# A two-layer graph transformer block on one core: row norms made chunk by chunk in the stages where their rows arise, the graph weight applied ahead of the aggregation, the output stored by chunks

## The reference

```python
xn = _layernorm(x)
x = x + _L0_gnn_ref(xn, src, dst, Wq, bq, Wk, bk) + _L0_mix_ref(xn, ...)
x = x + _L0_ffn_ref(_layernorm(x), ...)
xn = _layernorm(x)
x = x + _L1_gnn_ref(xn, edge_weight, W, b, src, dst) + _L1_mix_ref(xn, ...)
x = x + _L1_ffn_ref(_layernorm(x), ...)

def _L0_mix_ref(x, ...):            # t: linear attention over all rows
    x1 = layer_norm(t + x, ln1_g, ln1_b)
    h = gelu(x1 @ W1.T + b1)
    return layer_norm(h @ W2.T + b2 + x1, ln2_g, ln2_b)

def _L1_gnn_ref(x, edge_val, W, b, edge_row, edge_col):
    support = x @ W
    gathered = support[edge_col] * edge_val[:, None]
    return segment_sum(gathered, edge_row) + b

def _L1_mix_ref(x, ...):            # msg: linear attention over all rows
    msg = _layernorm(msg @ Wm, g1, b1)
    h = relu(concatenate([x, msg]) @ W1) @ W2
    return x + _layernorm(h, g2, b2)

def _L1_ffn_ref(x, ...):            # two experts, the same for every row
    return _layer_norm(sum_of_weighted_experts(x) + x, gamma, beta)
```

## Time and profile before

| | us |
|---|---|
| median of 3 runs | 7595.01 |
| profiled execution | 7602.24 |
| its span | 7600.5 |
| PE busy | 4920.3 (65%) |
| VectorE (DVE) busy | 3625.5 (48%) |
| ScalarE (ACT) busy | 2115.7 (28%) |
| GpSimd (POOL) busy | 4936.4 (65%) |

### The profile page before, as it was taken

How to read it: one execution, slowest core, us unless ns; L and a number is a source line. 1 busy time by engine, 2 the same in 40 slices (tenths; PEclk the granted TensorE clock), 3 DMA queues, 4 the chain that set the end, 5 groups by cost and what they waited for, 6 DMA issues and landing times. The chain is left out here.

```text
span 7600.5 us, 120043 instructions
## 1 busy us (share of the span) xinstructions
PE 4920.3 (65%) x21606; PEld 3536.8 (47%) x21607; DVE 3625.5 (48%) x12097; ACT 2115.7 (28%) x4904; POOL 4936.4 (65%) x5789
## 2 busy tenths in 40 slices
PE   0663436889999999719926639265656565655692
PEld 0333323555666666507813528244444444434582
DVE  8882545666667777731122330633333333333314
ACT  6321333445555555404423213000000000001450
POOL 0387377777777777567747667577777777772002
PEclk9886767999999999959968969678787878788896
DMA  3101003444444444300010000033333333331000
GB/s 85 38 2 11 6 4 89 116 116 116 116 116 116 116 116 116 81 3 15 3 38 4 4 12 3 14 106 105 106 105 105 106 106 105 106 105 41 13 0 35
DMA packets 504121, 493.93 MB, mean 65 GB/s; under 512 B 373899, under 2 KB 401027, under 8 KB 503299
## 3 DMA queue, kind: packets, MB, share of 16 engines
q0 software_dynamic: 200192, 432.72, 20.7%
q1 hardware_dynamic: 177155, 55.21, 3.4%
q10 hardware_dynamic: 126720, 5.46, 1.1%
HBM read 462.74 MB, written 30.23 MB: 65 GB/s over the span
## 5 line engine op out<-in xcount | busy, mean ns | idle before, releaser
L1060 POOL DMA_INDIRECT XN<-table,XN x3128 | 2988.8, 955 | 832.0 <-issue 704.5
L487 POOL DMA_INDIRECT records<-slot_rec,slot_pos x1564 | 1604.0, 1026 | 466.2 <-issue 466.2
L1374 PE MATMUL gcn_psE<-XN,gcn_pE 128*125 x3520 | 1187.7, 500 | 929.7 <-SPq L1040 914.6
L1374 PEld LDWEIGHTS gcn_psE<-XN,gcn_pE 128*125 128x125 f32 x3520 | 832.1, 246 | 1285.0 <-issue 1127.1
L1194 PE MATMUL gat_psE<-XN,gat_pE 128*125 x3520 | 876.0, 392 | 3.4 <-ACT gat_pE L1247 2.9
L1402 DVE TENSOR_TENSOR room<-room,gcn_psE 125x256 f32 x440 | 185.3, 421 | 1195.8 <-PE gcn_psE L1374 1194.5
L1194 PEld LDWEIGHTS gat_psE<-XN,gat_pE 128*125 128x125 f32 x3520 | 635.4, 191 | 84.4 <-issue 4.6
L73 POOL TENSOR_TENSOR cell<-cell 1x1 int32<-1x1 int32 x874 | 174.6, 200 | 657.8 <-DMA slot_pos<-spill_pos 613.9
L602 ACT ACTIVATE gcn_w_stage<-room 125x512 f32 (+1 forms) x25 | 15.6, 622 | 2082.5 <-PEq L115 2082.5
L539 POOL TENSOR_TENSOR X<-X,room x150 | 120.6, 836 | 620.8 <-DVE room L581 620.8
L1390 DVE TENSOR_SCALAR gcn_pE<-iota_n,gcn_lk,gcn_rec 128x125 f32<-128x125 f32 x1760 | 504.8, 359 | 16.0
(11 more groups left out here) (399 smaller groups left out, 7712.7 us busy)
## 6 DMA issues: line engine op xcount, KB each, us to landing
XN<-table,XN POOLq DMA_INDIRECT x3128, 2.8
records<-slot_rec,slot_pos POOLq DMA_INDIRECT x1564
XN<-records SPq DMA_DIRECT2D x782, 6.0 KB, 1.7
table<-XN SPq DMA_DIRECT2D x10, 1250.0 KB
gat_rec<-records ACTq DMA_DIRECT2D x440, 6.0 KB
gcn_rec<-records ACTq DMA_DIRECT2D x440, 6.0 KB
out_x<-X SPq DMA_DIRECT2D x5, 1250.0 KB
X<-in_x SPq DMA_DIRECT2D x1, 5600.0 KB
```

Source lines behind the costliest of these rows:

```text
L487: pool.indirect_dma_start(out=rec_d[self.which], out_offset=bass.IndirectOffsetOnAxis(ap=slot_pos[:, h, j:j + 1], axis=0), in_=slot_rec[:, ...
L1060: pool.indirect_dma_start(out=rows_t[:, s, j, :], out_offset=None, in_=table, in_offset=bass.IndirectOffsetOnAxis(ap=rec_g[:, s, j, 1:2].b ...
L1374: last = pe.matmul(psE[d][0:B, 0:D], pE[:, d, j, :], rows_t[:, slot_of(g), j, :].rearrange("p a w -> p (a w)"), start=(j == 0), stop=(j == ...
```

## The change

**Norms in place.** A class `RowNorm` gives VectorE the mean and 1/sqrt of the two blocks of a chunk. The stages ln_b, ln_c, ln_e, ln_f, ln_g and ln_i are gone: att0 norms its chunk behind the residual, mix0, ffn0, mix1 and ffn1 in their `final`, and `linear_norm` takes the place of `linear` for merge, reading the rows out of psY. `final` itself now raises `fin` where psY is free, and a new semaphore `done` tells that a chunk is through. Additions to X that GpSimd did are made by VectorE.

**Graph weight first.** sums1 also multiplies each chunk by L1_gnn_W; ScalarE copies the product and stores it as the table from which the edge stage gathers. The five stores of XN by SyncE are gone there. The edge sums go straight into X; the clearing of U ahead of them and the stage gcn_w are gone; the bias is added to the offset of the norm in mix1.

**Output.** ffn1 works on X, and SyncE stores each chunk as it is done, 25 stores in place of five.

**Turns** are now ln_a 1, sums0 6, att0 4, mix0 5, ln_d 2, topk 2, ffn0 9, sums1 5, att1 3, merge 3, mix1 6, again 46.

```diff
+        class RowNorm:
+            PER = 2 * CH + 14
...
+            def of(self, dve, st, rows_of):
+                st.mark(dve.tensor_copy(self.pace[:, 0:1], ones[0:B, 0:1]))
+                for b in range(CH):
+                    st.mark(dve.bn_stats(self.stats[:, b, :], rows_of(b)))
+                st.all()
+                st.mark(dve.tensor_copy(self.pace[:, 1:2], ones[0:B, 0:1]))
+                for b in range(CH):
+                    st.mark(dve.bn_aggr(self.mv[:, b, :], self.stats[:, b, :]))
+                st.all()
+                st(dve.tensor_scalar(self.var[:, :], self.mv[:, :, 1], LN_EPS, None, ALU.add))
+                st(dve.tensor_scalar(self.half[:, :], self.var[:, :].bitcast(I32), 1, None, ALU.logical_shift_right))
+                st(dve.tensor_scalar(self.guess[:, :], self.half[:, :], -1.0, float(0x5f3759df), ALU.mult, ALU.add))
+                for _ in range(3):
+                    st(dve.scalar_tensor_tensor(self.sq[:, :], self.r, -0.5, self.r, ALU.mult, ALU.mult))
+                    st(dve.tensor_tensor(self.sq[:, :], self.sq[:, :], self.var[:, :], ALU.mult))
+                    st(dve.scalar_tensor_tensor(self.r, self.sq[:, :], 1.5, self.r, ALU.add, ALU.mult))
...
                         with loop(dve, NC, st, per) as k:
+                            dve.wait_ge(done, k)
                             dve.wait_ge(y_mm, k + 1)
-                            final(dve, st, k, [p[0:B, :].rearrange("p (b d) -> p b d", b=CH) for p in psY], b2, tmp).then_inc(fin, 1)
...
+                            last = final(dve, st, k, [p[0:B, :].rearrange("p (b d) -> p b d", b=CH) for p in psY], b2, tmp, fin, norm, held_rows)
+                            last.then_inc(done, 1)
...
+                        with loop(dve, NC, st, norm.PER + 2 * CH - 1) as k:
                             dve.wait_ge(y_mm, k + 1)
-                            final(dve, st, k, psY[0:B, :].rearrange("p (b d) -> p b d", b=CH), b2).then_inc(fin, 1)
...
+                            norm.of(dve, st, lambda b: psY[0:B, b * D:(b + 1) * D])
+                            for b in range(CH):
+                                last = dve.scalar_tensor_tensor(one(U[:, bass.ds(k * CH + b, 1), :]), psY[0:B, b * D:(b + 1) * D], norm.mean(b),
+                                                                gain[:, :], ALU.subtract, ALU.mult)
+                                if b < CH - 1:
+                                    st.mark(last)
+                            last.then_inc(fin, 1)
+                            dve.wait_ge(fin, k + 1)
+                            for b in range(CH):
+                                u = one(U[:, bass.ds(k * CH + b, 1), :])
+                                st.mark(dve.scalar_tensor_tensor(u, u, norm.rstd(b), offset[:, :], ALU.mult, ALU.add))
+                            st.all()
...
                                 last.then_inc(qk_mm, 1)
+                            if proj is not None:
+                                pe.wait_ge(w_out, k)
+                                for b in range(CH):
+                                    for f in range(KF):
+                                        last = pe.matmul(psW[0:B, b * D:(b + 1) * D], xT[:, f, b * B:(b + 1) * B], wp[:, f, :],
+                                                         start=(f == 0), stop=(f == KF - 1))
+                                last.then_inc(w_mm, 1)
...
+                            if proj is not None:
+                                pe.wait_ge(w_out, k + 1)
...
+                            if proj is not None:
+                                act.wait_ge(w_mm, k + 1)
+                                act.wait_ge(w_stored, k * 16)
+                                act.activation(prod[:, :, :], psW[0:B, :].rearrange("p (b d) -> p b d", b=CH), ACT.Copy).then_inc(w_out, 1)
+                                act.wait_ge(w_out, k + 1)
+                                act.dma_start(rows(table)[:, bass.ds(k * CH, CH), :], prod[:, :, :]).then_inc(w_stored, 16)
...
+                            if affine:
+                                dve.wait_ge(fin, k + 1)
+                                u = U[:, bass.ds(k * CH, CH), :]
+                                st.all()
+                                st(dve.tensor_tensor(u, u, XN[0:B, bass.ds(k * CH, CH), :], ALU.add))
+                                norm.of(dve, st, lambda b: one(U[:, bass.ds(k * CH + b, 1), :]))
+                                for b in range(CH):
+                                    u = one(U[:, bass.ds(k * CH + b, 1), :])
+                                    st.mark(dve.scalar_tensor_tensor(u, u, norm.mean(b), gain[:, :], ALU.subtract, ALU.mult))
+                                st.all()
+                                for b in range(CH):
+                                    u = one(U[:, bass.ds(k * CH + b, 1), :])
+                                    st.mark(dve.scalar_tensor_tensor(u, u, norm.rstd(b), offset[:, :], ALU.mult, ALU.add))
+                                st.all()
...
-                    def _(dve):
-                        dve.memset(U[:, :, :], 0.0)
...
+                            ub = one(X[:, bass.ds(b, 1), :])
                             dve.wait_ge(used, t * RING + s + 1)
...
+        def scaled(dve, st, norm, dst, src_of, gain, offset, freed=None):
+            for b in range(CH):
+                last = dve.scalar_tensor_tensor(dst[:, b, :], src_of(b), norm.mean(b), gain[:, :], ALU.subtract, ALU.mult)
+                if b < CH - 1 or freed is None:
+                    st.mark(last)
+            if freed is not None:
+                last.then_inc(freed[0], 1)
+                dve.wait_ge(freed[0], freed[1])
+            st.all()
+            for b in range(CH):
+                st.mark(dve.scalar_tensor_tensor(dst[:, b, :], dst[:, b, :], norm.rstd(b), offset[:, :], ALU.mult, ALU.add))
+            st.all()
+        def twice_normed(dve, st, k, ys, b2, tmp, fin, norm, held):
+            dve.tensor_tensor(tmp[:, :, :], ys[0], b2[0][:, :].unsqueeze(1).broadcast_to([B, CH, D]), ALU.add).then_inc(fin, 1)
+            dve.wait_ge(fin, k + 1)
+            st(dve.tensor_tensor(tmp[:, :, :], tmp[:, :, :], U[:, bass.ds(k * CH, CH), :], ALU.add))
+            norm.of(dve, st, lambda b: tmp[:, b, :])
+            scaled(dve, st, norm, tmp, lambda b: tmp[:, b, :], held[0], held[1])
+            x = X[:, bass.ds(k * CH, CH), :]
+            return dve.tensor_tensor(x, x, tmp[:, :, :], ALU.add)
...
+                for b in range(CH):
+                    last = dve.tensor_scalar(one(XN[0:B, blk(k, b), :]), one(X[:, blk(k, b), :]), norm.mean(b), norm.rstd(b), ALU.subtract, ALU.mult)
+                    if b < CH - 1:
+                        st.mark(last)
+                return last
             mlp("ffn0", [XN], [(A["L0_ffn_w1"], A["L0_ffn_b1"], A["L0_ffn_w2"], A["L0_ffn_b2"].partition_broadcast(B))],
-                4 * D, ACT.Gelu_apprx_tanh, 1 + CH, weighted, turns=10)
+                4 * D, ACT.Gelu_apprx_tanh, RowNorm.PER + 2 * CH, weighted, turns=9)
             end_phase()
...
+        def into_x(dve, st, k, ys, b2, tmp, fin, norm, held):
+            x = X[:, bass.ds(k * CH, CH), :]
+            norm.of(dve, st, lambda b: ys[0][:, b, :])
+            scaled(dve, st, norm, tmp, lambda b: ys[0][:, b, :], held[0], held[1], (fin, k + 1))
+            st(dve.tensor_tensor(x, x, XN[0:B, bass.ds(k * CH, CH), :], ALU.add))
+            return dve.tensor_tensor(x, x, tmp[:, :, :], ALU.add)
...
+        def written(sp, done):
+            with loop(sp, NC) as k:
+                sp.wait_ge(done, k + 1)
+                sp.dma_start(rows(out)[:, bass.ds(k * CH, CH), :], X[:, bass.ds(k * CH, CH), :]).then_inc(s_out, 16)
+            sp.wait_ge(s_out, 16 * NC)
```

More of the change, by code:

```diff
@@ L659, in mlp @@
                 total = len(experts) * nf
+                done = sem(name + "_done")
+                norm = RowNorm(c, name + "_norm")
+                held_rows = [sb(c, f"{name}_row{i}", [B, D]) for i in range(len(extra))]
                 mv = mover(name, turns)
@@ L921, in attention_sums, with attention_rows @@
             return kvd
[L923 removed]
+        def attention_rows(name, wq_dram, kvd, affine=None, turns=0):
             with ExitStack() as c:
@@ L978, in _ @@
                         st = Steps(dve, own)
-                        with loop(dve, NC, st, 2 + CH if residual else 2) as k:
+                        dve.wait_ge(loaded, n_loads)
+                        with loop(dve, NC, st, 2 + 3 * CH - 1 + norm.PER + 1 if affine else 2) as k:
                             dve.wait_ge(q_mm, k + 1)
@@ L1708, in gps_kernel @@
         end_phase()
-        layer_norm("ln_i", U, U, affine=(A["L1_ffn_gamma"], A["L1_ffn_beta"]), into=X)
-        end_phase()
-        s_out = sem("out_written")
-        with nc.Block() as block:
-            @block.sync
-            def _(sp):
-                for i in range(5):
-                    n = NB // 5
```

(2 more changed lines are left out.)

154 lines of the change are left out of this document (85 added, 69 removed).

## The result

The changed kernel takes 7279.04 us in the median of 3 runs (7275.8 to 7284.11), the kernel before 7595.01. The ratio is 0.9587, with a 95% interval of 0.9565 to 0.9608. The profiled execution has a span of 7274.1 us, 326.4 less than the 7600.5 of before. Forecast were 7213 and a range of 7150 to 7285: the time lies in the range, 66 us above the forecast and near its upper end.

A forecast was written before the change was run, and what follows sets the result against it. Barriers close every stage, so the kernel is the sum of its stages, each lasting as long as its last engine (GpSimd in ffn0 and mix0). Terms per stage summed to -381.5: 7595 - 382 = 7213 us, range 7150 to 7285.

The forecast's parts named there:

- The price of a norm: In each chunk that takes a norm: statistics, pacing copies and 12 linked tiny steps cost VectorE 3.5 us.
- The clock: In att0 and merge: granted clock between 0.5 and 1, giving chunks of 12.1 and 7.6 us.
- I take the middle: In att0: a chunk of 12.1 us, between 11.65 and 12.6 at the lower clock; stage 311 us, +75.
- rival 1: att0 and merge both run at the lower clock: +38 us, 7251 us in all; chance 0.10.
- merge's mean of 0.69 with ln_f: Argument against the lower clock in att0 and merge: old merge and its norm stage averaged 0.69, half without PE.
- sums1: Stage with the added projection: 232 us against 236.5, -4.
- ScalarE's chunk is 7.65 at the full clock: In sums1: ScalarE's chunk of 7.65 us grows by 0.7 and 0.3 to 8.65, in all 216 us.
- rival 3: sums1 falls to a chain of 12.3 us per chunk at the lower clock: +84, 7297 us; chance 0.05.
- GpSimd's turns: Turns of 34 scatters: each moved turn counts 43 us where GpSimd is last, nothing where another engine is.
- Scatters beside norms: In mix0 and ffn0: scatters slightly slower beside norms, 9 us put down, with 0 and 22 as ends.
- rival 4: Norms hold up all 850 scatters of mix0, ffn0, sums1 and mix1: +399, 7612 us, slower than before; chance 0.02.
- What vanished without a counterpart: ln_g with the clearing (-115.8), gcn_w (-99.7) and the end with ln_i and output (-129.5): -345 us.

## Why the forecast was right, and where it was off

**The price of a norm** held. 3.56 us from the first pacing copy to the first pass with the mean in att0 and 3.70 in merge, forecast 3.5:

```profile
905.19 0.15 DVE L605 COPY att_norm_pace<-ones 125x1 f32<-125x1 f32 x1
...
908.75 0.88 DVE L1101 SCALAR_TENSOR_TENSOR room<-room,att_norm_mv,att_gain 125x256 f32 x2
...
911.08 0.74 DVE L1072 TENSOR_SCALAR att_e<-att_psQ 128x250 f32<-128x250 f32 x2 [0.53 <-DVE room L1105]
...
915.47 0.24 DVE L1081 TENSOR_SCALAR att_z<-att_psM 125x8 f32<-125x8 f32 x2 [2.21 <-PE att_psM L1051]
```

The sum itself writes 12 x 0.20 as 2.3; with 2.4 it is the 3.56 of att0. The same rows decide the clock: z comes 4.39 us after the first pass, the lower level's figure of the earlier trace rows. The chunk is 12.7 long on the mean of the stage, not 12.1.

**The clock** is the step that failed: "I take the middle" for att0, 7.6 for merge. There is no middle here; both stages are rival 1's, 12.6 and 8.6 forecast for it, 12.7 and 8.5 measured, and the eight matmuls on psM, for which z waits, took 2.12 us in each of att0's 25 chunks. That explains 38 of the 42 us of these two terms (25 x 0.5 and 25 x 1.0); the rest is mostly att0's first pass, which with two more loads comes 11.3 us after the stage's start instead of 8.2. The reason given against the rival, merge's mean of 0.69 with ln_f, was the wrong row: it is a mean over time and not over work, and of a stage in which PE did not yet wait for the norm. The one given for it was read too widely: ln_a in the earlier trace rows has 1.00 with PE doing nothing. The Trainium skill's page "TensorE: Matmul & The Clock Gate", section "HAM oscillation — how this bites in real kernels", says that pauses between bursts let the clock drop again and again. The trace agrees for the bursts that the next step waits for, 0.50 in merge's and in att0's on psM; the matmuls right behind the latter, on psQ, already ran in part at the full clock (0.78 over one of them). By that rule the term would have been right. The runs with the extra matmuls show that it is the pause.

**sums1** failed in its first row. "ScalarE's chunk is 7.65 at the full clock" was true of the chunk in the earlier trace rows, and all 25 were put at it. In the kernel before, the bursts on K and V already took turns between the two levels:

```profile
3979.28 3.65 PE L836 MATMUL sums_psKV<-sums_wkv,sums_xT 128*125 128x512 f32 x8
...
3987.12 5.09 PE L836 MATMUL sums_psKV<-sums_wkv,sums_xT 128*125 128x512 f32 x8
...
3996.22 3.65 PE L836 MATMUL sums_psKV<-sums_wkv,sums_xT 128*125 128x512 f32 x8
```

12 of the 25 took 5 us or more, and the mean chunk 8.52 us. In the changed kernel 11 of 25 did, and the mean chunk is 9.56: the growth of 1.04 per chunk is about the 1.0 that was forecast, and no more bursts are low than before. The stage grew by 12 us and not by 25, because what follows the start of the last burst shrank from 25.7 to 12.0 us. So the low bursts, for which rival 3 stood with 12.3 us for all chunks, are the reason that the stage lies above its forecast, but the change didn't bring them. They also come without a long pause: PE's longest wait in such a chunk is 1.02 us.

**GpSimd's turns** were read rightly where they bound: ffn0 412.0 for 414.6 forecast, ln_a 51.5 for 51, mix0 241.9 for 239; in mix0 VectorE ended 24 us ahead of the stage's end, and the run with a turn less gave just that. The old att0 was read at a fast chunk too, 5.91 us where the mean is 6.58, but nothing hangs on that except the start of the loop.

**Scatters beside norms** (rival 4) came to nothing: 0.971 us in ffn0 and 1.001 in mix0, where the rival wanted 1.45:

```profile
L487 POOL DMA_INDIRECT records<-slot_rec,slot_pos x306 | 297.2, 971 | 91.0 <-issue 91.0
...
L487 POOL DMA_INDIRECT records<-slot_rec,slot_pos x170 | 170.2, 1001 | 50.7 <-issue 50.7
```

**What vanished without a counterpart** gave 347 us where 345 were forecast: ln_g, the clearing, gcn_w and the end (5 of the 347 are the edge sums' own); PE stays the bound of ffn1 and the output is hidden in it but for the last store. The rest of the change, the norms folded into chunks and sums1, gave +26 where -36 were forecast, and the stages that are the same -5. Two of its folds are losses that the prediction's own sums could have shown: it compared merge with its old stage at two turns and with ln_f at two, but not with the same number of turns put elsewhere.

What stays open is the last 10 us: the medians lie 316 apart, the profiled executions 326.

## What to carry to other kernels

Fold a step into a chunk loop only where another engine bounds that loop: in mix1 and ffn1 the stages grew by 11 and 14 us, where a norm stage had taken 85 to 116. In att0 and merge the folds cost 90 and 60 us until reordering (-74) and a second PSUM tile (-64) gave them something to lie under. Even then the two only break even: merge takes 157.8 us against 162.4 for the two stages apart, att0 255.4 with five turns against 239.6 with four. Read a chunk's time as the mean of the loop, not off one chunk. Before filling an engine's waits, ask what the wait does to the clock of the bursts behind it, and read the clock over the bursts, not over the stage. A DMA that is issued from a compute engine's queue holds up everything behind it until its source is ready (2.15 us in sums1); whether issuing it one chunk late pays by itself was not measured apart from the table load.
